# Second GRU layer of a two-layer graph network: products of h2 issued before the transposes of the neighbour sums

## What is computed

```python
h = jnp.maximum(_layernorm(x, axis=-1), 0.0)
msg = h[edge_src] + relvectors[edge_rel]
red = jax.ops.segment_sum(msg, edge_dst, num_segments=h.shape[0])
gi = red @ w_ih.T + b_ih          # the sum's products
gh = h @ w_hh.T + b_hh            # the row's own products
i_r, i_z, i_n = jnp.split(gi, 3, axis=-1)
h_r, h_z, h_n = jnp.split(gh, 3, axis=-1)
r = jax.nn.sigmoid(i_r + h_r)
z = jax.nn.sigmoid(i_z + h_z)
n = jnp.tanh(i_n + r * h_n)
x = x + (1.0 - z) * n + z * h
```

## Time and profile before

| what | value |
|---|---|
| time, median of 3 runs | 1218.3 us (1218.26 to 1241.45) |
| profiled execution, its time | 1217.22 us |
| profiled execution, its span from the first to the last instruction | 1215.6 us |
| PE busy | 853.1 us (70%) |
| DVE busy | 682.5 us (56%) |
| POOL busy | 563.5 us (46%), none of it in the last third |
| ACT busy | 293.9 us (24%) |
| mean granted clock of TensorE over the span | 0.704 of full speed |

### The profile page before, as it was taken

The page is one execution under the profiler, slowest core; times in us unless marked ns, Lnnn a source line. Parts: engine busy times, 40 slices in busy tenths (PEclk is TensorE's granted clock), DMA queues, the critical chain, the costliest instruction groups (busy, mean ns, idle before and its releaser), DMA issues.

```text
span 1215.6 us, 14336 instructions
## 1 busy us (share of the span) xinstructions
PE 853.1 (70%) x5247; PEld 640.5 (53%) x5247; DVE 682.5 (56%) x1264; ACT 293.9 (24%) x621; POOL 563.5 (46%) x495
## 2 busy tenths in 40 slices
PE   0451656667655666665556666569999999999997
PEld 0341444456544455544445555446666666676764
DVE  4452566664565664455556555545566666555562
ACT  5230111111111111111111111224333333344331
POOL 3537277787778787777787877300000000000000
PEclk9985655555555555555555555569999999999999
DMA  4226233334333333332333331000000000000000
GB/s 126 79 48 128 81 72 69 73 79 95 73 70 71 73 81 82 78 68 68 71 71 74 80 84 35 12 13 18 17 15 16 13 18 17 18 17 18 18 14 14
DMA packets 42545, 65.97 MB, mean 54 GB/s; under 512 B 14247, under 2 KB 31696, under 8 KB 39350
## 3 DMA queue, kind: packets, MB, share of 16 engines
q1 hardware_dynamic: 24843, 48.23, 12.0%
q0 software_dynamic: 16576, 16.76, 11.0%
q10 hardware_dynamic: 1056, 0.07, 0.1%
HBM read 57.69 MB, written 7.20 MB: 53 GB/s over the span
## 4 chain that ended last, share of the span: by engine, by line
POOL 42%; PE 35%; issue 13%; DVE 4%; SPq 3%; DMA 2%; ACT 1%; POOLq 0%; DVEq 0%; ACTq 0%
POOL shared L638 40%; PE bank L1671 11%; PE bank L1670 5%; PE bank L1714 4%; PE bank L1721 4%; PE bank L1655 3%; PE bank L1722 2%; PE bank L1715 2%; DVE layer L1076 1%; DVE layer L1078 1%; POOL oh L712 1%; PE bank L1519 1%; PE bank L1682 1%; DMA layer<-in_edges,row_at 1%; DMA rels<-in_L_gnn_relvectors 1%
## 5 line engine op out<-in xcount | busy, mean ns | idle before, releaser
L638 POOL DMA_INDIRECT shared<-zu_table,sidx x450 | 534.5, 1188 | 162.9 <-issue 136.5
L1623 PE MATMUL bank<-layer,oh 128*125 128x84 f32 x900 | 192.1, 412 | 0.0
L1623 PEld LDWEIGHTS bank<-layer,oh 128*125 128x125 f32 x900 | 187.9, 326 | 0.0
L1600 PE MATMUL bank<-zu,shared 125*128 125x64 bf16 x1350 | 85.3, 238 | 78.8 <-issue 43.5
L1600 PEld LDWEIGHTS bank<-zu,shared 125*128 125x128 bf16 x1350 | 74.7, 127 | 102.4 <-issue 102.3
L1038 DVE TENSOR_SCALAR den<-bank 125x4 f32<-125x4 f32 x25 | 4.1, 162 | 189.9 <-issue 129.7
L1609 PE MATMUL bank<-ident,L 128*72 128x128 f32 x75 | 21.0, 417 | 125.6 <-DVE L L957 68.8
L1076 DVE COPY layer<-bank 125x256 f32<-125x256 f32 x25 | 10.6, 424 | 141.0 <-PE bank L1671 141.0
L907 DVE TENSOR_TENSOR shared<-iota_b,key_col 128x3125 bf16<-128x3125 bf16 x25 | 85.2, 3409 | 0.0
L907 DVE TENSOR_TENSOR oh<-iota_b,low_col 128x3125 bf16<-128x3125 bf16 x25 | 85.2, 3409 | 0.0
L1609 PEld LDWEIGHTS bank<-ident,L 128*72 128x72 f32 x75 | 9.4, 159 | 135.6 <-DVE L L957 73.8
(11 more groups left out here) (227 smaller groups left out, 1513.4 us busy)
## 6 DMA issues: line engine op xcount, KB each, us to landing
shared<-in_edges SPq DMA_DIRECT2D x25, 1125.0 KB
shared<-zu_table,sidx POOLq DMA_INDIRECT x450
xs<-in_x SPq DMA_DIRECT2D x5, 625.0 KB
h_table<-h2s SPq DMA_DIRECT2D x25, 125.0 KB
h2s<-h_table SPq DMA_DIRECT2D x25, 125.0 KB
out_dram<-layer SPq DMA_DIRECT2D x25, 125.0 KB
halo_i<-in_edges SPq DMA_DIRECT2D x25, 108.6 KB
zu_table<-zus SPq DMA_DIRECT2D x5, 156.2 KB
```

The costliest lines, as they stand in the source:

```text
L638: nc.gpsimd.indirect_dma_start(out=to(h, j), out_offset=None, in_=table, in_offset=bass.IndirectOffsetOnAxis(ap=sidx[:, h, j:j + 1], axis= ...
L1600: last = mm(ps(c, 128, (j - a) * KR, (j - a + 1) * KR), ohT[:, j * 128:(j + 1) * 128], zu3[:, m, :], start=m == 0, stop=m == 2)
L1623: last = mm(ps(5, W, 0, SUMS), oh[:, h, j * W:(j + 1) * W], V[:, j, :], start=j == 0, stop=j == C - 1)
```

## The change

In `gru` of the PE program `row_gates` moves ahead of the transposes of the neighbour sum. The wait for `h2T_kept` that stood ahead of the transposes goes with it (`row_gates` has its own, the first of its two in a window of before). The other engines' programs are untouched, and so is every operation's shape. Below the changed place the lines are numbered one lower: L1714 of before is L1713 after.

```diff
                 turn_rows(t, i, h)
                 packed_gates(t, h)
+                row_gates(t, h)
                 pe.wait_ge(sum_kept, 2 * t + 2)
-                pe.wait_ge(h2T_kept, t + 1)
                 for c in range(CH):
                     last = tr(ps(6, 128, (CH + c) * W, (CH + c + 1) * W), redS[:, c * 128:(c + 1) * 128], ident[0:W, 0:W])
                 last.then_inc(sum_turned, 1)
-                row_gates(t, h)
                 gates(t, h)
```

## The result

| | before | after |
|---|---|---|
| median of the runs beside each other | 1220.15 us (1217.34 to 1241.45) | 1245.84 us (1239.92 to 1267.34) |
| ratio, with its 95% interval | | 1.0215 (1.0149 to 1.028) |
| profiled execution | 1217.22 us | 1240.71 us |
| its span | 1215.6 us | 1239.0 us |
| first sum product (L1671) starts at | 794.2 us | 798.7 us |

One run of each six, 1241.45 and 1267.34 us, took over 1.5% longer than the fastest of its kernel and is left out of the ratio.

The account below looks back on a forecast made before the run. PE bounds layer 1, with 15.95 us of work in a 16.10 us stretch. 24 windows at 0.64 us plus 0.45 for the last add 15.8 us to 1218.3: 1234.1 us, 1.3% slower, range 1230 to 1240.

Parts of the forecast that it names:

- The mechanism: At a window's end in layer 1, own products moved ahead uncover the sum's trip through ACT: 0.07 us gained, 0.71 paid.
- Rival 1: Clock falls in PE's new gaps, kernel over 2% slower; once in every window adds 45 us, giving 1279 us; chance 0.05.
- rival 3: The sum's trip through ACT hides after all, leaving only the earlier start: 1.9 us, 1216.4 us; chance 0.04.
- Rival 2: The sum's trip through ACT costs more than its pieces, over 0.98 us a window, so 1243 us or more; chance 0.03.
- psum-queue rule: Skill's page: frequent short PE idles between matmul groups make the clock go back and forth; held not to fit this kernel.
- the hand-over to a matmul: At PE's two waits, matmul starts 0.03 and 0.02 us behind its weights; as a bound 0.10 us.
- start of the block, earlier by: Own products start when h2T is there, 0.07 us before the transposes started: 1010.31 for 1010.38.
- own products, to the first transpose: Block of own products on PE, now ahead of the transposes, takes 2.59 us.
- first transpose to the first product of the sums: Sum's trip through ACT: 0.50 to the copy, 0.38 copy, 0.05 hand-over, 0.02 to the matmul, 0.95 us together.
- a window, more than before: Each layer 1 window gets 0.64 us longer, 0.07 gained and 0.71 paid; the last costs 0.45 us.
- from layer 1 to the median: Layer 1's added 15.8 us goes straight onto the 1218.3 us median, 1.1 us above the profiled execution.
- the upper bound: Matmuls at both waits start 0.10 us behind their weights: 0.80 us a window, 20 us, 1238.3 us.

Follow-up runs that it names:

- e3: Changed kernel with half of the own products ahead of the transposes of the sums, half behind them: ratio 0.9995 to the kernel before, a window 16.08 us.
- e5: Kernel before with ACT copying the transposed sum twice, first into a spare tile: ratio 0.9995 to the kernel before.
- e6: Changed kernel with ACT copying the transposed sum twice, first into a spare tile: ratio 1.0205 to the kernel before, a window 17.08 us.
- e7: Changed kernel with ACT's copy of the transposed sum in two halves, each with its own bank and wait: ratio 1.0112 to the kernel before, a window 16.60 us.
- e4: Changed kernel with half the own products ahead of the sums' transposes, half behind, and h2's transposes moved into the sum loop: ratio 1.0032 to the kernel before.
- e8: Changed kernel with own products split around the sums' transposes, h2 transposed inside the sum loop, next window's count products later: ratio 0.9963 to the kernel before, 1211.97 us.

## Why the prediction was wrong

**The mechanism stood.** The trip of the sum through ACT had been covered by the own products, and moving them ahead uncovered it: e3, e5, e6 and e7 show this. It gave back next to nothing, by the trace 0.09 us a window. Rival 1 (the clock) and rival 3 (the trip hides) did not happen. Rival 2 was right in its number and not in its cause: the median is over its 1243 us, but a window lost 0.77 us and not 0.98. On the psum-queue rule of the Trainium skill that stood in the prediction, this trace sides with the row of this kernel: a gap of 0.53 us in each of 25 windows, PE busy 16.29 of 16.87 us, and 1.00 throughout. (The prediction says that by this rule the time would be longer by what "the second rival" gives; the price meant is that of the first, 45 us. Its reading of the earlier trace rows also passes over the first three slices, whose clock digits are 9, 9 and 8.)

The median of after lies 11.7 us above the forecast. 3.3 us of that are the trip, mis-sized in the sum; 1.9 us are the kernel before, which itself stood at 1220.15 us and not 1218.3 in this measurement; 6.6 us are what the changed kernel took beyond layer 1, which the sum put at nothing. Two steps failed, then, and the second is the larger.

**The first step that failed is the hand-over to a matmul: I took 0.03 and 0.02 us from weights to matmul, and kept 0.10 as a bound.** The start times alone agree: L1720's weights and matmul both start at 1027.71. But the first of its two matmuls then takes 0.53 us until the second starts, where 0.43 us is the rule: the row's two together have 1.12 us, the second alone 0.59; behind another matmul two have 1.02 (1024.12 and 1027.71 above, against 1010.62 of the earlier trace rows and 1012.12 in e3). I read this as a matmul that starts together with the load of its own weights and waits for that load inside its own time; the rows show the 0.10 us and the common start, not the waiting itself. The rows of a window, term by term:

| term | taken | measured |
|---|---|---|
| start of the block, earlier by | 0.07 | 0.09 |
| own products, to the first transpose | 2.59 | 2.68 |
| first transpose to the first product of the sums | 0.95 | 0.91 |
| products of the sums, more than before | 0 | 0.10 |
| a window, more than before | 0.64 | 0.77 |

The 0.09: DVE's addition ended at 1023.71 + 0.42 = 1024.13, so in the old order the transposes would have started at about 1024.21, 0.08 us later as in the earlier trace rows; the own products started at 1024.12. The measured 2.68 is 1026.80 - 1024.12, with 0.10 us of the same kind at its first matmul, and 0.91 is 1027.71 - 1026.80. The block of before lasts 2.83 us from the first transpose to the products of the sums (1010.38 to 1013.21), so: 2.68 + 0.91 + 0.10 - 2.83 - 0.09 = 0.77. Times 24, and some 0.6 for the last window (18.3 us between the spans of the transposes, less 23 x 0.77), it is 19.1 us; the two traces differ by 18.9 us in layer 1 (440.3 less 421.4). I had 15.8. That alone would have put the median at 1237.4, within the range.

The Trainium skill bears on this: on its page "TensorE: Matmul & The Clock Gate", under "Step-by-step: what each phase is for", PE pulls weight loads ahead of matmuls in flight, so that the next tile's weights load while this one's matmul runs. The trace agrees: after the change the weights of the products of the sums had to wait for redT and loaded with their matmul (1027.71 above); before it they loaded 0.22 us ahead, as the timeline of before has it:

```profile
1012.99 0.40 PEld L1721 LDWEIGHTS bank<-wihT,layer 128*125 128x125 f32 x2
1013.21 1.02 PE L1721 MATMUL bank<-wihT,layer 128*125 128x512 f32 x2
```

**The second step that failed is the one from layer 1 to the median: layer 0 and the scatter of a measurement were put at nothing.** The 1.7 us between the upper bound and the end of the range were for the moment at which the clock rises. The first trace of after came into layer 1 4.5 us later than that of before, and its median was 25.7 us above the other's. Three measurements gave 1.0215, 1.0151 and 1.0165; the 19 us of layer 1 are 1.0156 of 1217 us, inside all three intervals. The range was made around a single profiled execution, and had no term for how much layer 0, on which nothing changed, varies: it ended between 788.1 and 798.7 us in these traces, and single runs of the changed kernel took between 1229.91 and 1238.86 us in the two later measurements.

Two things set the first measurement apart from all later ones. First, the clock. In its two traces TensorE was granted 0.50 from 200 to 780 us (1.2 GHz throughout), in the nine later traces 0.59 to 0.61 (the higher level at times); over the whole span all six of its runs of the changed kernel have 0.703 to 0.709, and no later run of any kernel is under 0.74. Second, in its trace of after POOL, whose gathers (L638) have the largest share of any line in the chain of waits (40% before, 33% after), waited twice for the indices that DVE makes. The waits from 100 to 800 us (total us, times, longest), before and then after:

```profile
POOL shared L638 <- DVE sidx L963: 21.4, 1, 21.4
```

```profile
POOL shared L638 <- DVE sidx L963: 28.2, 2, 20.8
```

The nine later traces have this wait once, for 16.8 to 17.7 us. The second one of after, 7.43 us, ends at 527.45 us, and in the same trace DVE, which makes the indices after this row, stood before it for 9.04 us, for a releaser that the profile does not name:

```profile
520.67 0.68 DVE L995 TENSOR_TENSOR_SCAN runs<-cutf,bank 72x256 f32<-72x256 f32 x1 [9.04 <-remote]
...
527.45 3.32 POOL L638 DMA_INDIRECT shared<-zu_table,sidx  x1 [7.43 <-DVE sidx L963]
```

That is more than the 4.5 us by which layer 1 began later. Whether the lower clock is behind this wait, and what lifted all runs of that measurement (1239.92 us and more), no run here shows: the low clock did not come back, and the kernel before lost only some 4 us with it.

**What the profile was to show.** The 25 waits for the copy to redT came, 19.0 us in 25 of them, 0.76 each where I had said some 0.9; the transposes came 2.7 us behind the start of the own products for 2.6; a window 16.87 us for 16.7; the clock stood at 1.00 from 814.4 us on, later than 810 as layer 1 began later. That DVE "has 6 us free in a window" was true and misled: it has them after the mixing, while from the end of the sums to the first count products it has none, as e4 and e8 show. It did not bear on this change, which only made that stretch longer.

## What to carry to other kernels

Before independent work is moved ahead of a hand-over to another engine, ask what lies behind it: work between handing over and needing the result can cover the whole round trip. Here a start 0.09 us earlier was bought with a trip of 0.91 us, of which only the 0.24 us of the transposes had been paid before. Split such work, so that each wait has some: half of it (1.29 us) covered the trip as well as all of it. When a single execution is the base of a forecast, ask for a second one before the range is drawn: here the part that the change did not touch varied by 10 us. And once PE really waits, add the load of the weights to the wait, 0.10 us for each such place here, though no row shows it as idle time.

## What was not expected

- The first fp32 matmul of 512 columns behind a wait took 0.53 us instead of 0.43 until the next one started. The same 0.10 us appears where nothing was waited for: in e8 the own products follow the packed products, whose weights have 51 rows and not 128, and h2T had been there for 1.6 us; the timeline of e8:

```profile
1009.60 0.64 PE L1706 MATMUL bank<-relw,cnt_rows 51*125 51x512 bf16 x2
1010.17 0.29 PEld L1719 LDWEIGHTS bank<-whhT,layer 128*125 128x125 f32 x2 [0.39 <-issue]
1010.17 1.12 PE L1719 MATMUL bank<-whhT,layer 128*125 128x512 f32 x2
```

  So the weights can come late without a wait too. Whether the change of height is the cause was not tried.
- Two copies of 250 columns behind each other on ACT start 0.27 to 0.28 us apart, while each has a duration of 0.38: a row's duration overstates by some 0.10 us what one more of them costs. The Trainium skill's page "ScalarE: Activation LUTs", section "What ACT_TABLE_LOAD costs", says that back-to-back ACTIVATEs overlap by about 93 ns; the rows of e5 and e6 agree.
- Two chains of the kernel before are of the same length to within what the trace shows: PE's own work from the end of the sums to the first count products, and DVE's one-hots. Shortening PE's alone gave nothing (e4). Shortening DVE's alone was not tried.
